# Gated cross-attention and MLA/MoE block: one transpose for a group's maxima, and the last value product moved beside the spread

## The reference, cut to what matters

```python
x = x + tanh(g_xattn) * xattn(layernorm(x), ctx, ctx, mask)   # pass A
x = x + tanh(g_ffn) * ffn(layernorm(x))                        # passes B and C

# xattn: 16 heads of 32
scores = einsum('bhqd,bkhd->bhqk', Q, K) / sqrt(32) + rel_bias[h, clip(q - k)]
scores = where(key_padding_mask, -inf, scores)
out = einsum('bhqk,bkhd->bqhd', softmax(scores), V) @ Wo + bo

# ffn: attention, then experts
att = einsum('bhqd,bhkd->bhqk', q, k) / 8        # 16 heads of 64, half of them rotated
att = softmax(where(tril, att, -inf))
y = einsum('bhqk,bhkd->bhqd', att, v) @ Wo
x = x + y;  out = x + moe(rmsnorm(x))
```

## Time and profile before

| | us |
|---|---|
| runs, median (lowest to highest, of 3) | 2419.53 (2417.91 to 2424.08) |
| the profiled execution, its own time | 2419.89 |
| its span, first to last instruction | 2418.0 |
| TensorE busy | 2171.5, 90% of the span |
| VectorE, ScalarE, GpSimd busy | 1514.7, 1197.2, 1365.2 |
| pass A, TensorE's last value product of the group loop | about 903 |
| pass B, first to last value product | about 1025 to 1810 |

### The profile page before, as it was taken

How to read it: one execution, slowest core, us unless ns; L and a number is a source line. 1 busy time by engine, 2 the same in 40 slices (tenths; PEclk the granted TensorE clock), 3 DMA queues, 4 the chain that set the end, 5 groups by cost and what they waited for, 6 DMA issues and landing times. The chain is left out here.

```text
span 2418.0 us, 50305 instructions
## 1 busy us (share of the span) xinstructions
PE 2171.5 (90%) x12864; PEld 982.9 (41%) x12865; DVE 1514.7 (63%) x4218; ACT 1197.2 (50%) x2316; POOL 1365.2 (56%) x1452
## 2 busy tenths in 40 slices
PE   3899999999999963899999999999985797899997
PEld 1333333333333311344444444444432343455554
DVE  3788888887888843556565565555533678344443
ACT  3355555554555442355545454454544574455554
POOL 3267677677677670264655564565561565455554
PEclk7999999999999986899999999999997899899999
DMA  5413323232232203543434353352414576666665
GB/s 173 147 57 107 97 86 110 70 110 87 96 106 75 80 9 129 146 118 117 147 94 135 101 154 117 101 156 88 134 50 136 86 178 132 106 114 114 111 109 91
DMA packets 221402, 264.60 MB, mean 109 GB/s; under 512 B 37400, under 2 KB 163468, under 8 KB 220852
## 3 DMA queue, kind: packets, MB, share of 16 engines
q1 hardware_dynamic: 197612, 212.79, 29.2%
q0 software_dynamic: 22976, 48.38, 11.6%
q10 hardware_dynamic: 536, 0.28, 0.0%
HBM read 162.12 MB, written 86.80 MB: 103 GB/s over the span
## 5 line engine op out<-in xcount | busy, mean ns | idle before, releaser
L497 ACT ACTIVATE a_pt<-a_bank 128x512 f32<-128x512 f32 x512 | 305.1, 597 | 356.2 <-DVE a_bank L604 343.5
L1384 DVE CUSTOM_DVE_ANT_0 b_bank<-b_bank,b_tri 128x256 f32<-128x256 f32 (+3 forms) x512 | 253.7, 497 | 322.7 <-PE b_bank L1522 320.3
L615 DVE CUSTOM_DVE_ANT_0 a_bank<-a_bank,a_strip 128x512 f32<-128x512 f32 x512 | 354.2, 693 | 7.3 <-PE a_bank L760 4.6
L1169 POOL TENSOR_TENSOR b_acc<-b_acc,b_pt 128x256 f32<-128x256 f32 (+2 forms) x384 | 271.7, 725 | 104.6 <-ACT b_pt L1258 88.0
L407 POOL TENSOR_TENSOR a_acc<-a_acc,a_pt 128x512 f32<-128x512 f32 x256 | 317.8, 1270 | 14.6 <-ACT a_pt L497 11.3
L604 DVE TENSOR_TENSOR a_bank<-a_bank,a_band 128x256 f32<-128x256 f32 (+1 forms) x512 | 205.6, 402 | 132.0 <-PE a_bank L747 130.2
L1258 ACT ACTIVATE b_pt<-b_bank 128x256 f32<-128x256 f32 (+2 forms) x384 | 143.4, 381 | 202.1 <-PE b_bank L1506 199.0
L747 PE MATMUL a_bank<-a_q_stack,a_k_stack 128*128 128x512 f16 x512 | 197.7, 388 | 14.6 <-ACT a_pt L497 10.2
L760 PE MATMUL a_bank<-a_k_stack,a_q_stack 97*128 97x512 f16 x512 | 196.3, 384 | 3.6 <-DVE a_low L615 3.5
L1850 POOL DMA_INDIRECT out_dram<-c_z,c_to_row x72 | 114.1, 1585 | 139.6 <-DMA out_dram<-c_z,c_to_row 106.5
L1504 PE MATMUL b_bank<-b_q_stack,b_k_stack 96*128 96x256 f16 (+3 forms) x512 | 155.5, 304 | 9.5 <-ACT b_pt L1258 6.4
(11 more groups left out here) (346 smaller groups left out, 5501.8 us busy)
## 6 DMA issues: line engine op xcount, KB each, us to landing
b_q_stack<-qk_rows SPq DMA_DIRECT2D x192, 128.0 KB, 2.7
a_q_stack<-qk_rows SPq DMA_DIRECT2D x96, 128.0 KB
a_k_stack<-qk_rows SPq DMA_DIRECT2D x96, 128.0 KB
b_k_stack<-qk_rows SPq DMA_DIRECT2D x96, 128.0 KB, 2.6
a_sums<-in_x SPq DMA_DIRECT2D x34, 256.0 KB, 3.2
qk_rows<-a_qk_hi SPq DMA_DIRECT2D x64, 128.0 KB, 1.7
qk_rows<-a_qk_lo SPq DMA_DIRECT2D x64, 128.0 KB, 1.8
out_dram<-a_sums SPq DMA_DIRECT2D x32, 256.0 KB, 2.0
```

The lines of the kernel that those rows point to most:

```text
L497: nc.scalar.activation(pt[:, n % SLOTS, :], st_bank[n % 2][:], ACT.Exp).then_inc(exped, 1)
L615: nc.vector.tensor_tensor_reduce(out=max_bank[step % 2][:], in0=max_bank[step % 2][:], in1=strip[:, g * HG + hh, at:at + S], scale=-1.0, s ...
L1169: nc.gpsimd.tensor_tensor(sums_of, sums_of, probs(n), ALU.add).then_inc(pooled, 1)
L1384: nc.vector.tensor_tensor_reduce(out=max_bank[step % 2][:, 0:w], in0=max_bank[step % 2][:, 0:w], in1=tri[:, at:at + w], scale=-1.0, scalar ...
```

## The change

Two edits, the same in both passes.

First, the order of the columns in `low` becomes `hh * NT + i`, and one transpose turns all 16 columns of a group at once, into 16 rows of 128. `m_row` takes that form, ScalarE's copy and the DMA follow, and the DMA's source, read row by row, gives the same order of values as before.

Second, `fill` is called twice per step: before the value product for all jobs but the spread, and after it for the spread alone. The value product of key tile 3 is done in step 8 instead of 7, between the two calls, so that it stands right ahead of the spread. ScalarE's copy of `out_bank` moves from step 8 to step 9. The diff, of pass A, with the one hunk of pass B that reads otherwise:

```diff
@@ -105,7 +105,7 @@
-        m_row = sb("m_row", [HG, 2, S], F16)
+        m_row = sb("m_row", [NT * HG, 2, P], F16)
@@ -476,7 +476,7 @@
-                    nc.scalar.activation(m_row[:, n % 2, :], src[0:HG, :], ACT.Copy).then_inc(left_act, 1)
+                    nc.scalar.activation(m_row[:, n % 2, :], src[0:NT * HG, 0:P], ACT.Copy).then_inc(left_act, 1)
@@ -516,8 +516,8 @@
-                        if off == 8:
-                            act.wait_ge(summed, b * (UNITS // HG) + (step - 8) // HG)
+                        if off == 9:
+                            act.wait_ge(summed, b * (UNITS // HG) + (step - 9) // HG)
@@ -615,7 +615,7 @@
-                                                       accum_out=low[:, g % 2, i * HG + hh:i * HG + hh + 1]).then_inc(lowered, 1)
+                                                       accum_out=low[:, g % 2, hh * NT + i:hh * NT + i + 1]).then_inc(lowered, 1)
@@ -707,14 +707,12 @@
                 pe.wait_ge(lowered, b * UNITS + (g + 1) * GS)
-                for i in range(NT):
-                    last = nc.tensor.transpose(bank_of(kind, job)[0:HG, i * P:(i + 1) * P], low[:, g % 2, i * HG:(i + 1) * HG], idn[:])
-                last.then_inc(job_done, 1)
-
-            def fill(kind, b, step):
+                nc.tensor.transpose(bank_of(kind, job)[0:NT * HG, 0:P], low[:, g % 2, :], idn[:]).then_inc(job_done, 1)
+
+            def fill(kind, b, step, spreads):
 
                 for job in names:
-                    if job not in present[kind]:
+                    if job not in present[kind] or (job[0] == SP) != spreads:
                         continue
@@ -759,9 +757,10 @@
-                    fill(kind, b, step)
-                    n = step - L - 2
-                    if has_unit(kind, n) and n % HG == HG - 1:
+                    fill(kind, b, step, False)
+                    beside = (step - L - 2) % GS == 0
+                    n = step - L - 2 - beside
+                    if has_unit(kind, n) and n % HG == HG - 1 and (beside or n % GS != GS - 1):
                         g, j = divmod(n // HG, NT)
@@ -774,6 +773,7 @@
                         last.then_inc(summed, 1)
+                    fill(kind, b, step, True)
@@ -1465,18 +1465,17 @@
                     pe.wait_ge(lowered, b * UNITS + (n + 1) * GS)
-                    for i in range(NT):
-                        last = nc.tensor.transpose(o[0:HG, i * P:(i + 1) * P], low[:, n % 2, i * HG:(i + 1) * HG], idn[:])
+                    last = nc.tensor.transpose(o[0:NT * HG, 0:P], low[:, n % 2, :], idn[:])
```

## The result

The changed kernel takes **2403.8 us** (median; 2402.8 to 2406.5), the kernel before beside it 2419.8 (2417.9 to 2424.1): a ratio of 0.993, 95% interval 0.9915 to 0.9946. The profiled execution took 2406.5 us, at a span of 2404.7.

What follows compares the result with a forecast made beforehand. TensorE was taken as the bound, busy 99.4 of 100 us in pass A and 96.0 in pass B. Pass A 2.1 us slower and pass B 11.6 faster gave 9.5 faster, 2419.9 to 2410.4 us; range 2403 to 2421.

Steps and rivals of the forecast that it cites:

- the two named places: Pass A, steps 8 and 24: first (V, 3) and (O, 3) pieces wait for VectorE, 1.48 and 1.11 us.
- the release of a waiting product: TensorE product freed by VectorE: taken to start 0.20 us after VectorE's work ends.
- The transpose: Both passes, per group: one transpose costs 0.108 us, three go, 0.32 us saved; ScalarE's copy and DMA cost 0.
- the eaten one at b_qu_lo: Pass B, step 33: a 0.95 us wait for VectorE grows by 0.32, eating one transpose gain in seven batches.
- The joined blocks: Value product and spread blocks back to back: 0.18 us saved per joint, between 0 and 0.23.
- What the move uncovers: Value product moved behind step 8's other work (mod 16): new pass A waits of 1.48 and 1.11 us, none in pass B.
- Sum, pass A: Per steady batch 2.0 us gained, 2.6 lost; with first and last batches, pass A 2.1 us slower.
- Sum, pass B: No new wait; 1.68 us gained per steady batch, 1.5 in first and last batches: pass B 11.6 us faster.
- Rival 1: Pass A's new waits do not come; 15.5 us return, 2395 us; chance 0.08.
- Rival 2: The clock falls behind each of pass A's twelve new waits, 20 us lost, 2431 us; chance 0.07.
- Rival 3: Joints of blocks save nothing: 10.1 us less gain, 2420.5 us; chance 0.08.
- rival 4: Other waits eat more of the gains in both passes: 3.8 us faster remain, 2416 us; chance 0.12.

Runs made afterwards that it cites:

- the repeat: The changed kernel measured and profiled once more with no edit, against the kernel before: 2405.0 us, ratio 0.9938.
- the broken joint: Changed kernel, but in pass B a group's last value product stands ahead of the maxima product, parted from the spread: 2408.3 us, ratio 0.9953.
- the transpose alone: The kernel before with only the first edit, one transpose of 16 columns; value products and spreads as before: 2401.0 us, ratio 0.9928.
- the joined blocks alone: The changed kernel with the four transposes of four columns and the old `low` put back: 2417.0 us, ratio 0.9993.
- the kernel with the cover given back: Changed kernel, but in pass A value product and spread, where side by side, come ahead of the other pieces: 2388.3 us, ratio 0.9871.

## Where the prediction failed, and what of it held

Its mechanisms held: faster, by both passes' slots, with twelve new waits of pass A at the two named places. It forecast 9.5 us and 16 came, 14.5 in the repeat; the first lies just outside the range, the second (2404.5 by its ratio) just inside. Two terms of its sum were mis-sized, the joint of two blocks (0.18 for 0.23 us) and the release of a waiting product (0.20 for 0.05 to 0.06), and both made the changed kernel too slow. With them the sign of pass A's sum was wrong: 2.1 us slower was forecast, and the pass is 5.5 shorter (3.2 in the second profile). So one of its own signs of being wrong, pass A shorter by over 5 us, came true in the first profile; but 3.4 and 3.9 us of that are clock falls at the loops' ends, which the sum left out. Its steps in turn:

- **The transpose.** 0.108 forecast, 0.109 found, and the eaten one at b_qu_lo 1.27 forecast, 1.28 found. ScalarE's copy and DMA cost nothing that the periods show.
- **The joined blocks.** Mis-sized: 0.18 forecast, 0.23 measured, the upper bound. I charged the joint 0.02 to 0.03 over streaming. In the profile of after the second block starts 0.43 after the last round of the first, the streaming time itself (behind the dots the row of the second block's weight loads):

```profile
325.38 0.61 PE L773 MATMUL a_bank<-a_pt,a_v 128*32 128x512 f32 x4
325.81 0.61 PE L702 MATMUL a_bank<-a_acc,a_ones_f 128*32 128x512 f32 x4
...
325.38 0.13 PEld L702 LDWEIGHTS a_bank<-a_acc,a_ones_f 128*32 128x32 f32 x4 [0.30 <-issue]
```

  The 0.02 to 0.03 came from the 0.45 between the two rounds of a block that stood alone. In after the first of two joined blocks has that 0.45 too (324.93 to 325.38), the second only 0.43 (325.81 to 326.24), so it is part of getting in. The rule of the Trainium skill that I set against it (TensorE: Matmul & The Clock Gate, Part 3: weights overlap matmuls in flight only in another row group) does not hold here: the spread's weight loads (PEld) start at 325.38, while the last round of the value product streams on the same rows, and the broken joint in pass B costs 0.245. The 0.05 missed make up to 3 us over 64 joints.
- **What the move uncovers.** Right in place and cause, 1.48 and 1.11 forecast, 1.33 and 0.97 found. The failed number is the release: I took 0.20 from the end of VectorE's work to TensorE's start out of a row where the product had only come in its turn, 0.22 behind the one before it, and waited for nothing. The release itself shows in the trace of before in the weight load of the same product (PEld), which did wait and started 0.06 after VectorE's end at 325.32:

```profile
325.38 0.10 PEld L693 LDWEIGHTS a_bank<-a_w_hi,a_o_hi 128*128 128x128 f16 x1 [0.20 <-DVE a_ct_lo L579]
```

  Where TensorE does wait in after, 0.05 to 0.06 pass. That is 0.14 for each of twelve waits, 1.7 us.
- **Sum, pass A.** "2.1 slower" was 2.1 faster in the first profile and 0.7 slower in the second, loops' ends left out. A steady batch was forecast 0.6 slower and is 0.04 slower in both: 3.4 us, nearly all of it the two sizes above. In the first and last batches, forecast 1.5 faster, the interval that leads into the last batch fell from 98.38 to 96.47 us in both profiles, where "I take 0.3" assumed that GpSimd's additions would take back what was saved. Of the other stretches there nothing can be said: behind that interval the pass is 0.4 shorter in one profile and 1.0 longer in the other. My sign for pass A hung on a difference of 2.6 and 2.0 us, both known to a tenth at best, and the text should have said so.
- **Sum, pass B.** 11.6 forecast, 14.0 found in the first profile and 15.6 in the second, loops' ends left out. 1.68 a steady batch forecast, 1.83 found, 0.9 us over six; the first and last batches gave 3.1 and 4.7 where I took 1.5 (the table above has the sixth interval, the one behind batch zero, among those, with 1.8).
- **Rival 1**, no new waits, fell in the trace. **Rival 2** fell: the clock stayed at 1.00 from 100 to 850 us, with all twelve new waits in it. **Rival 3** fell by the broken joint, and **rival 4** by the transpose alone, where all four transposes of a steady batch of pass A come through and pass B loses 0.13 of 0.98.

So 4.3 of the 6.6 us missed in the first profile lie in steady batches, by the sizes of joint and release. The rest lies in the first and last ones, and only in part repeats. All steady terms erred to one side; the range was made as if they could not add up. That the direction came out right for the whole is owed to pass B, whose forecast gain was over five times the loss forecast for pass A.

## What to carry to other kernels

When a block of work moves behind a piece that waits for another engine, it stops covering that wait. Put it back ahead of the piece, in the same step: here this is worth 14 us by the periods (2.34 in each of six batches) and 17 by the medians, as much as the whole change, for a few lines. Price a release from rows where the engine, or its weight load, is marked as waiting, and an effect inside a loop from the period of one iteration, which repeats to 0.03 us when the program's time does not to 8.

## What the runs showed that I had not expected

**The length of a wait does not decide the clock behind it.** At the two ends of the loop in pass A and the two in pass B, TensorE waits 1.6 to 3.2 us, mostly with no releaser in the trace ("issue"), whatever the kernel. In the transpose alone and in the joined blocks alone two of these waits are alike:

```profile
585.52 0.39 PE L745 MATMUL a_bank<-a_q_stack,a_k_stack 128*128 128x512 f16 x1 [1.93 <-issue]
...
585.50:589.50 4.00, 3.98 (x11) 1.43 (x12) 2.28 (x6) 1.34 (x3) 2.61 (x3) 0.60 0.18 54
```

and, in the joined blocks alone:

```profile
598.18 0.39 PE L747 MATMUL a_bank<-a_q_stack,a_k_stack 128*128 128x512 f16 x1 [1.90 <-issue]
...
598.20:602.20 4.00, 4.00 (x21) 1.92 (x22) 3.09 (x8) 2.03 (x4) 3.00 (x3) 1.00 0.41 112
```

Behind the first the granted clock is 0.60 of full (most of the 4 us at 1.2 GHz), behind the second 1.00. The kernel before has a wait of 1.90 too, at 594.48, and behind that one 0.57. In after it fell at one of four ends:

```profile
591.03 0.39 PE L745 MATMUL a_bank<-a_q_stack,a_k_stack 128*128 128x512 f16 x1 [2.09 <-issue]
...
1508.54 0.39 PE L1503 MATMUL b_bank<-b_q_stack,b_k_stack 96*128 96x256 f16 x1 [3.04 <-issue]
...
591.00:595.00 4.00, 3.96 (x19) 1.79 (x20) 2.92 (x10) 1.75 (x4) 2.88 (x3) 1.00 0.21 57
...
1509.00:1513.00 4.00, 4.00 (x14) 1.76 (x12) 0.76 (x2) 1.03 (x3) 1.75 (x4) 0.50 0.85 278
```

In pass A an end with a fall adds 3.6 to 3.9 us to its batch, one without 1.8 to 2.4: a fall costs about 1.8. Before had three in its four ends, the other kernels' profiles none to two. Two falls against none are 3.6 us, about what the table gives pass A at its loops' ends. Whether the kernel before falls more often, or its one trace was unlucky, stays open; with four ends a fall more or less moves one execution by some 2 us each, which is a good part of the scatter of single runs. Whether the waits at the ends of pass B really got longer in after (2.37 and 3.04, before 2.00, behind ScalarE's exponential, and 2.26) is open as well: the kernel with the cover given back has the same pass B as after, and waits 2.31 and 2.48.
